# Attention scores: transposed tiles move to four PSUM banks, row scores keep two

## The reference

```python
x = x + 0.5 * _L0_ffn_ref(_layernorm(x, axis=-1), ...)
x = x + _L0_attn_ref(_layernorm(x, axis=-1), ...)          # Mamba
x = x + 0.5 * _L0_ffn_ref(_layernorm(x, axis=-1), ...)
x = x + 0.5 * _L1_ffn_ref(_layernorm(x, axis=-1), ...)
x = x + _L1_attn_ref(_layernorm(x, axis=-1), L1_attn_Wq, ...)
x = x + 0.5 * _L1_ffn_ref(_layernorm(x, axis=-1), ...)

# _L1_attn_ref, after q, k, v = projections, and RoPE on q and k
logits = jnp.einsum('bhqd,bhkd->bhqk', q, k) * scale
logits = jnp.where(causal[None, None], logits, jnp.finfo(logits.dtype).min)
attn = jax.nn.softmax(logits, axis=-1)
out = jnp.einsum('bhqk,bhkd->bhqd', attn, v)
return out.transpose(0, 2, 1, 3).reshape(bsz, q_len, NH * HD) @ Wo.T
```

## Time and profile before

| what | value |
|---|---|
| median of three runs | 2533.43 us (2530.44 to 5908.05) |
| profiled execution | 2539.86 us, of which the span is 2538.0 us |
| PE busy | 2358.7 us, 93% of the span |
| PE weight loads busy | 1812.6 us, 71% |
| DVE busy | 1660.0 us, 65% |
| ACT busy | 1311.4 us, 52% |
| POOL busy | 1330.1 us, 52% |
| mean granted TensorE clock | 0.958 of full speed |

### The profile page before, as it was taken

The page is one execution under the profiler, slowest core; times in us unless marked ns, Lnnn a source line. Parts: engine busy times, 40 slices in busy tenths (PEclk is TensorE's granted clock), DMA queues, the critical chain, the costliest instruction groups (busy, mean ns, idle before and its releaser), DMA issues. The chain is left out here.

```text
span 2538.0 us, 33152 instructions
## 1 busy us (share of the span) xinstructions
PE 2358.7 (93%) x12442; PEld 1812.6 (71%) x12442; DVE 1660.0 (65%) x2163; ACT 1311.4 (52%) x1905; POOL 1330.1 (52%) x876
## 2 busy tenths in 40 slices
PE   6997899999999999999999999999889977877876
PEld 5875788888888888888888888887668744554433
DVE  6555787687687588588588588678365345664414
ACT  3214576577477477477477467567323132234423
POOL 2221498598599499499489589579422200000000
PEclk9998899999999999999999999999889988869988
DMA  5321333233233233233223333232143202000001
GB/s 134 96 73 54 107 113 104 87 110 103 86 102 117 79 112 113 79 108 108 88 92 117 90 102 112 88 100 84 42 116 88 65 14 79 1 2 1 3 1 47
DMA packets 163406, 204.07 MB, mean 80 GB/s; under 512 B 24396, under 2 KB 86224, under 8 KB 163120
## 3 DMA queue, kind: packets, MB, share of 16 engines
q1 hardware_dynamic: 163248, 201.96, 26.5%
HBM read 198.43 MB, written 3.15 MB: 79 GB/s over the span
## 5 line engine op out<-in xcount | busy, mean ns | idle before, releaser
L1914 POOL TENSOR_TENSOR mamba_w_lo<-mamba_raw,mamba_w_hi 128x512 fp32r<-128x512 f32 x272 | 435.8, 1611 | 292.0 <-ACT mamba_w_hi L1742 292.0
L76 PE MATMUL psum<-mamba_hT_lo,mamba_w_hi 128*128 128x512 f32 x1152 | 461.9, 401 | 3.0 <-DVE mamba_bc L2005 3.0
L78 PE MATMUL psum<-mamba_hT_hi,mamba_w_lo 128*128 128x512 f32 x1152 | 456.3, 396 | 0.0
L77 PE MATMUL psum<-mamba_hT_hi,mamba_w_hi 128*128 128x512 f32 x1152 | 456.1, 396 | 0.0
L1933 POOL TENSOR_SCALAR mamba_L<-mamba_A,mamba_ts 128x256 f32<-128x256 f32 (+1 forms) x256 | 335.0, 1322 | 0.1
L2037 DVE TENSOR_TENSOR mamba_L<-mamba_L,mamba_cb 128x1536 f32<-128x1536 f32 x128 | 302.8, 2366 | 22.8 <-ACT mamba_L L1791 14.3
L2005 DVE SCALAR_TENSOR_TENSOR mamba_hid<-psum,mamba_cw,mamba_hid 128x1022 f32<-128x1022 f32 (+2 forms) x192 | 245.1, 1277 | 19.4 <-ACT mamba_hid L1749 14.8
L76 PEld LDWEIGHTS psum<-mamba_hT_lo,mamba_w_hi 128*128 128x128 f32 x1152 | 217.0, 188 | 53.2 <-DVE mamba_bc L2005 3.3
L78 PEld LDWEIGHTS psum<-mamba_hT_hi,mamba_w_lo 128*128 128x128 f32 x1152 | 216.7, 188 | 52.4
L77 PEld LDWEIGHTS psum<-mamba_hT_hi,mamba_w_hi 128*128 128x128 f32 x1152 | 217.1, 188 | 49.1
L2064 DVE SCALAR_TENSOR_TENSOR mamba_zs_lo<-mamba_z,mamba_dgn,mamba_zs_hi 128x512 fp32r<-128x512 f32 x128 | 117.4, 922 | 172.2 <-ACT mamba_zs_hi L1814 172.2
(11 more groups left out here) (281 smaller groups left out, 4945.7 us busy)
## 6 DMA issues: line engine op xcount, KB each, us to landing
mamba_A<-mamba_a_dram SPq DMA_DIRECT2D x128, 512.0 KB, 4.5
mamba_raw<-in_win SPq DMA_DIRECT2D x144, 256.0 KB, 2.6
mamba_raw<-in_wout SPq DMA_DIRECT2D x128, 256.0 KB, 2.6
mamba_Eb<-mamba_e_dram SPq DMA_DIRECT2D x128, 128.0 KB, 3.0
ffn_raw<-in_w SPq DMA_DIRECT2D x80, 128.0 KB, 3.6
ffn_scl<-in_s SPq DMA_DIRECT2D x80, 128.0 KB, 3.7
ffn_scl<-in_s SPq DMA_DIRECT2D x86, 64.0 KB, 2.3
ffn_raw<-in_w SPq DMA_DIRECT2D x20, 256.0 KB, 2.6
```

The costliest lines, as they stand in the source:

```text
L76: e.matmul(out, wh, ml, start=start, stop=False)
L77: e.matmul(out, wh, mh, start=False, stop=False)
L78: return e.matmul(out, wl, mh, start=False, stop=stop)
L1914: e.tensor_tensor(w.lo[:, k % NSPLIT, :], raw[:, k % NRAW, :], w.hi_read[:, k % NSPLIT, :], ALU.subtract).then_inc(s["w_lo"], 1)
```

## The change

Turned scores go to four banks, 2 and 3 for one pair and 4 and 5 for the next, in turn; so a pair waits for the `exp` of the pair before the last (`exped` at k - 2 instead of k, where k counts banks), and the first two pairs wait for none. Row scores give up banks 2 and 3: every pair of heads goes to banks 0 and 1 and waits for the maxima of the pair just before it. No product, `exp`, maximum or transfer is added or removed.

```diff
@@ score @@
-                    if k >= 2:
-                        e.wait_ge(peaked, k - 1)
+                    if k:
+                        e.wait_ge(peaked, k)
                     for h in range(2):
-                        e.matmul(psum[:, 2 * (k % 2) + h, 0:n], qs[HALVES[h], b, z, qt * P:(qt + 1) * P],
+                        e.matmul(psum[:, h, 0:n], qs[HALVES[h], b, z, qt * P:(qt + 1) * P],
                                  ks[HALVES[h], b, 2 * (z // QPK) + h, 0:n], start=True, stop=False)
                     for j in range(2):
                         for h in range(2):
-                            last = e.matmul(psum[:, 2 * (k % 2) + h, n - P:n],
+                            last = e.matmul(psum[:, h, n - P:n],
@@ score_t @@
-                    if k:
-                        e.wait_ge(exped, k)
+                    if k >= 4:
+                        e.wait_ge(exped, k - 2)
-                    outs = [ps[4 + h].rearrange("p (h q) -> p h q", h=QPK) for h in range(2)]
+                    outs = [ps[2 + k % 4 + h].rearrange("p (h q) -> p h q", h=QPK) for h in range(2)]
@@ exponential @@
-                    e.activation(pt[:, k % NPT, :], ps[4 + k % 2], ACT.Exp, scale=SCALE).then_inc(exped, 1)
+                    e.activation(pt[:, k % NPT, :], ps[2 + k % 4], ACT.Exp, scale=SCALE).then_inc(exped, 1)
@@ peak @@
-                                psum[:, 2 * (k % 2):2 * (k % 2) + 2, 0:n], AX.X, ALU.max).then_inc(peaked, 1)
+                                psum[:, 0:2, 0:n], AX.X, ALU.max).then_inc(peaked, 1)
```

## The result

The changed kernel takes 2589.66 us (median of four, 2584.53 to 2590.87) against 2534.66 us before: a ratio of 1.0219 with a 95% interval of 1.0197 to 1.0241, or 55 us slower. Whether it is more than 2% slower, the interval leaves open; that it is slower is clear. One execution of the kernel before took 5908.05 us, for which no trace gives a reason; without it the median before is 2533.43 us. The forecast was 38 us slower, 2571, with a range up to 2588. The direction was right, the size was not, and the time lies just outside the range.

The account below looks back on a forecast made before the run. DVE bounds the prefix; in the loop no engine is full and PE waits in a ring with ACT. Prefix +36.7 and loop +1.0 (-2.9 + 1.3 + 6.6 - 4.0) give +38: 2571 us, 8-in-10 range 2554 to 2588.

Parts of the forecast that it names:

- the prefix: 32 pairs of row scores before the loop: PE and DVE times add up, 78.1 us against 41.4, +36.7 us.
- Rival 1: The prefix runs at full clock: +23.5 there, kernel about +25, 2558 us; chance 0.13.
- the new ring: Loop: a quad's second row score waits for the maximum of the first, 1.56 us in steps 0-1.
- the term was +1.3: Steps 2-3, 12 quads: quads of two pairs gain, quads of three lose; +1.3 us in sum.
- 6.6 over before, which was the term: Steps 4-5, 8 quads of four pairs: three rings in each quad make them longer, +6.6 us.
- a ring: Steps 4-5: PE's start to DVE's start 0.49, maximum 0.42, back 0.05, together 0.96 us, three a quad.
- the term of -2.9: Steps 0-1, 16 quads: plain quads 3.33 against 3.45 us, masked 3.57 against 3.93; -2.9 us in sum.
- the clock of the loop: Loop: the sum leaves the granted clock as before, 0.97 in steps 2-3 and 0.95 in steps 4-5.
- rival 2: New waits bring half clock in steps 2 to 5, adding 34 us, 2605 us; chance 0.13.
- The rule named against the change: Cycling through PSUM banks can idle PE so often that its clock swings; by it rival 2 would be likely.
- The term was -4.0: Steps 6-7, no row scores: PE's waits for ACT go, -4.0 us, between 0 and -4.7.

Follow-up runs that it names:

- the prefix experiment: The changed kernel with the prefix's row scores on banks 0-1 and 2-3 in turn as before, loop of the change, profiled three times; 2541.06 us, ratio 1.0049.
- The filled kernel: The changed kernel plus four unread 512-column products before the second and fourth row score of each quad in steps 4-5; 2568.27 us, ratio 1.0134.

## Why the prediction was wrong

**Right: the prefix.** A round was worked out as 2.45 us at half clock and is 2.44; the term was +36.7, the trace has +36.1, and with the prefix changed alone the timed kernel loses 34 us. That DVE, which bounds the prefix, would stand still for as long as PE works, and that nothing hides it, came as said. Rival 1, full clock in the prefix, did not come: after about three rounds of 2.00 us the clock was at half, 0.53 in the mean. (The 0.73 us of a full-clock round are in no row of before; the changed kernel shows 0.72 for it, so the forecast's 2.01 stands.)

**Right: the new ring.** The waits for ACT are gone and those for DVE stand in their place. With the clock at 1.00, which the third profile of the prefix experiment gave in steps 2-3, that stretch takes 62.8 us, 1.4 over before; the term was +1.3. The other 2.9 of its 4.3 us go with the clock of 0.95. The filled kernel's steps 4-5 take 55.0 us at 1.00, 6.6 over before, which was the term. But before had 0.97 and 0.95 in these two stretches. At a clock of 1.00 the code of before takes 46.4 us in steps 4-5, so at equal clock the rings cost 8.6 there and not 6.6; that the sum met the number 6.6 is luck. The next point has the difference.

**A small error: a ring is 0.1 us longer.** Three rings a quad in eight quads make 24 of them in steps 4-5, some 2 us. The forecast took the time from PE's start to DVE's start from row scores that had not waited. The timeline of the changed kernel at the start of step 4 shows both kinds:

```profile
2410.22 0.19 PEld L1034 LDWEIGHTS psum<-attn_ks,attn_qs 64*128 64x128 f32 x2
2410.45 0.23 PE L1034 MATMUL psum<-attn_ks,attn_qs 64*128 64x128 f32 x2
...
2410.94 0.43 DVE L1247 TENSOR_REDUCE attn_mx<-psum 128x2 f32<-128x256 f32 x1 [0.16 <-PE psum L1038]
...
2411.42 0.19 PEld L1034 LDWEIGHTS psum<-attn_ks,attn_qs 64*128 64x128 f32 x2 [0.67 <-DVE attn_mx L1247]
2411.42 0.33 PE L1034 MATMUL psum<-attn_ks,attn_qs 64*128 64x128 f32 x2 [0.53 <-DVE attn_mx L1247]
...
2412.01 0.42 DVE L1247 TENSOR_REDUCE attn_mx<-psum 128x2 f32<-128x256 f32 x1 [0.65 <-PE psum L1038]
...
2412.49 0.33 PE L1034 MATMUL psum<-attn_ks,attn_qs 64*128 64x128 f32 x2 [0.24 <-DVE attn_mx L1247]
```

The first score, which did not wait, is handed to DVE after 0.49 us, the second, which did, after 0.59. The rows show where the time goes: the first one's weight load ran 0.23 us ahead of its product, beside the products before, and the second one's starts only with its product, behind the same wait. So the ring is 2412.49 - 2411.42 = 1.07 us where the forecast had 0.96. In steps 0-1 the same happens: a plain quad at full clock takes 3.44 to 3.45 us, exactly what it took before, where 3.33 was forecast. Those 12 quads gain nothing:

```profile
2298.15 0.50 PE L1061 MATMUL psum<-attn_qs,attn_ks 64*128 64x512 f32 x2
...
2300.05 0.44 PE L1034 MATMUL psum<-attn_ks,attn_qs 64*128 64x384 f32 x2 [0.77 <-DVE attn_mx L1247]
...
2301.59 0.50 PE L1061 MATMUL psum<-attn_qs,attn_ks 64*128 64x512 f32 x2
```

That steps 0-1 still came out 3.3 us shorter is their clock, 0.88 against 0.85, and the four masked quads; the term of -2.9 met the measured number partly by luck. The code of before took 68.5 us in another run at 0.93.

**The step that failed: the clock of the loop.** The sum left it "as it is", that is, it put the clock's cost at nothing, on the ground that PE already idled for a fifth of the time and its 41 short waits for ACT had not brought half clock. The trace of before does not bear that ground out. Behind the loop's first 12.8 us it has half clock again and again:

```profile
2256.50:2427.00 170.50, 136.06 (x1152) 77.93 (x1144) 71.78 (x123) 82.24 (x154) 0.00 (x0) 0.95 0.01 2
2268.00:2272.00 4.00, 3.33 (x18) 1.46 (x18) 1.80 (x2) 1.70 (x4) 0.00 (x0) 0.59 0.00 0
```

A mean of 0.95 over 170.5 us is an estimate of 17 us at half clock, and steps 6-7, with 4 of the 41 waits, had 0.79. Besides, those waits stood once a quad. The change puts up to three into each quad of steps 4-5 (20 in 8 quads stand in the waits, 0.47 us in the mean). The clock was full when step 4 began and fell during its first quad: behind waits of 0.53, 0.24 and 0.52 us the products that start at 2413.57 take 0.48 us, where those before took 0.33. Read in slices of 4 us, it then goes back and forth:

```profile
2414.00:2418.00 4.00, 3.29 (x18) 1.20 (x16) 0.43 (x1) 0.58 (x1) 0.00 (x0) 0.50 0.00 1
2418.00:2422.00 4.00, 3.48 (x25) 3.01 (x26) 1.53 (x4) 1.08 (x2) 0.00 (x0) 0.50 0.00 0
2422.00:2426.00 4.00, 3.47 (x25) 1.50 (x21) 0.85 (x2) 1.08 (x2) 0.00 (x0) 0.50 0.02 4
2426.00:2430.00 4.00, 3.24 (x30) 2.28 (x26) 0.85 (x2) 2.32 (x5) 0.00 (x0) 0.86 0.00 0
2430.00:2434.00 4.00, 3.48 (x17) 1.42 (x16) 0.85 (x2) 0.93 (x2) 0.00 (x0) 0.57 0.00 0
2434.00:2438.00 4.00, 4.00 (x7) 1.59 (x6) 0.00 (x0) 0.00 (x0) 0.00 (x0) 0.58 0.00 0
2438.00:2442.00 4.00, 2.61 (x21) 1.46 (x19) 1.79 (x4) 0.82 (x2) 0.00 (x0) 1.00 0.00 0
```

What the runs show in place of nothing is 16.2 us: the change takes 71.2 in this stretch, and 55.0 with the same rings and the gaps filled. With the rings' 8.6, and less the 2.0 that before lost to its own clock (48.4 against 46.4), that makes the 22.8. This is rival 2, in 8 of its 20 quads, about the number that it said would be enough to pass 2%. It had 1.94 us for each of these quads, 8 x 1.94 = 15.5, close to the 16.2. But that price was for half clock throughout, and a mean of 0.71 over 71.2 us is an estimate of 41 us at half clock; the stretch also holds the products of the output, which the rival did not count. So the mechanism of the rival came, and its number is right partly by luck. The busy shares in steps 4-5 hide this: PE is busy for 58.67 of 71.20 us, 82%, after 84% before, since products at half clock are busy for longer.

The rule named against the change in the prediction was the better guide. The Trainium skill ("TensorE: Matmul & The Clock Gate", "A second HAM failure mode: psum-queue depth-cycling") says that small gaps between groups of products, from cycling through PSUM banks, can make the clock swing; the seven rows above, and the filled gaps at 1.00, agree. In steps 2-3, with 19 waits of 0.6 us in 12 quads, it held only in part, 0.95 to 1.00.

**Steps 6-7.** The term was -4.0 with -4.7 as its bound, which counted the waits only. It was -9.7. With the waits gone the clock rose from 0.79 to 0.91 too. This is no accident of one profile: the three profiles with turned scores on two banks there have 0.79 to 0.84, the eleven with four banks 0.91 to 1.00. It is the same term, the clock put at nothing, with the other sign.

**What stays open.** The medians differ by 55 us, the stretches of the profiles by 50; and the changed kernel is 49 us over the version with the four-bank prefix in the medians, where the prefix is worth 36. The profiles of that version between 2544 and 2557 us show that the clock of the loop differs between executions of one program by this much, but the timed executions have no trace, so this is likely and not shown. Nor do the runs tell which part of standing still counts, how often PE does it or how long in all: the version with one wait a quad and the filled one lower both.

## What to carry to other kernels

A wait that is traded for another on PE has two prices: the wait, which the timeline gives, and what the engine's standing still does to its clock, which a sum of waits and busy times leaves out. Count how often PE would stand still in each turn of the loop, look in the trace of before for half clock behind such waits, and give the case a real chance when their number rises. Where a buffer must shrink, let one wait serve several pieces of work: here four pairs of heads side by side in the same two banks cost one wait of PE and one instruction of DVE, and turned a loss of 22.8 us into a gain of 7.5 (5.5 against the code of before at full clock).

## What was not expected of the hardware

- Work that nobody needs made the changed kernel 21 us faster, about 16 of them in the stretch that it fills: 64 products of 512 columns, put where PE waited about 0.5 us at a time, held the granted clock at 1.00 where it had been 0.71.
- The clock of a stretch differs between profiles though its code does not. Steps 0-1 with the code of before took 73.5, 73.6 and 73.5 us at 0.85 behind the short prefix and 68.5 at 0.93 behind the long one. Those of the change took 70.2 us at 0.88 and 73.6 at 0.83 behind the same long prefix, and 69.7 to 72.8 in three profiles of one program behind the short one. Whether the moment at which a stretch starts decides it is not shown. Differences below some 5 us between two profiles say little here unless their clocks agree.
- A row score behind a semaphore wait is handed over 0.1 us later than one that runs on without a wait, 0.59 against 0.49 us (n = 128, full clock).
